# Four stages in one program: where the last rows of a stage are normalised, and how the gate and up weights are loaded

## The chip, the cores and the metric

The kernel runs on one core of a Trainium2 chip. The metric is the device time of one execution in microseconds (us). The engines are TensorE (PE; its weight loads are shown apart as PEld), VectorE (DVE), ScalarE (ACT), GpSimd (POOL) and SyncE (SP, which here only issues DMAs and counts up semaphores); each runs its own queue of instructions in order and waits for the others by semaphores.

## The reference, cut to what matters

64 sequences of 64 tokens, width 256, go through two decoder layers of three sublayers each; after every sublayer the sum with its input is layer-normalised over the 256 columns.

```python
x = _layernorm(x + _L0_attn_ref(x, Wq, Wk, Wv, Wo))           # 16 heads of 128
x = _layernorm(x + _L0_xattn_ref(x, ctx_2048, ...))           # 16 heads, context and own rows
x = _layernorm(x + _L0_ffn_ref(x, w_gate, w_up, w_down))      # silu(x @ gate) * (x @ up) @ down, hidden 1024
x = _layernorm(x + _L1_attn_ref(x, ...))                      # 4-bit weights and activations
x = _layernorm(x + _L1_xattn_ref(x, ctx_2048, ctx_2048, ...))
x = _layernorm(x + _L1_ffn_ref(x, input2, scale, scale1))     # fp8 product
```

`_layernorm` subtracts the mean and divides by the square root of the variance plus 1e-5.

## The kernel before

All 4096 rows of x lie in SBUF as 32 tiles of 128 rows (`sh.x`, 128 partitions x 32 x 256). `program` (L3449) runs four stages one after the other: `self_attention_block` (A, 2 tiles per turn, 16 turns), `cross_attention_block` (B, 1 tile per turn, 32 turns), `gated_mlp_block` (C, 4 tiles per turn, 8 turns) and `tail_block` (D, all three sublayers of the second layer, 2 tiles per turn). Each stage is a block with its own instruction queues: all engines meet at its end before the next begins. The order inside a turn is written out by hand per engine (`turn`), and two or three turns overlap; the first and last turns are unrolled, the others are a loop.

The end of a turn is the same in A, B and C. `residual` (L104) adds the last projection to `sh.x` on VectorE into a buffer `res`; `row_stats` (L113) makes `bn_stats` and `bn_aggr` of each tile on VectorE; `normalise` (L130) makes five GpSimd steps: variance plus epsilon, the power -0.5, mean times that, rows times that, rows minus the shift, written back to `sh.x`. The buffers are `sh.res` (two tiles) in A and B, and `WideRows` (four tiles, allocated inside C) in C. For the last turn all of this stands at the end of the stage.

At its start B loads a context tile and its weights, VectorE lays out rotary tables, and GpSimd counts up 50 semaphores (L1168). C issues three loads of 1 MB each (`w_gateT`, `w_upT`, `w_downT`, L1318), counts up its semaphores on SyncE (L1320), copies four tiles of x (L1432), turns them on TensorE (L1330) and takes a high and a low part; ScalarE makes the high part of each weight (`split_high`, L66), VectorE the low part (`split_low`, L73), for three whole pieces in a row. `gate_up(i, j)` multiplies hidden columns 128 j to 128 j + 127; the first two (j = 0, 1) run before the loop once both gate and up are ready, the rest once `w_down` is. The last turn of C also rounds the second layer's weights (`sh.quantised`).

D first loads tile 0 and 1 of x and `of_chunk` by DMA (L1700, L1701). TensorE multiplies the value bias by the output weights (L1749), VectorE adds the output bias (L2254), TensorE waits for `of_chunk_ready` and turns x (L1762). Each turn starts with a chain that goes from engine to engine: `lowest` and `highest` (L2269, L2263, VectorE), `find_bias`, `halve_bias`, `find_spans` (L3022 to L3038, GpSimd), `widest` (L2282), `turn_cmax` (TensorE), `find_top`, `thresholds` (L2314), `exceed` (L2329, VectorE), `weigh_steps` (L3046, GpSimd) and on to the projections. GpSimd first clears the value buffers of both attentions (L2998 to L3013).

## Time and profile before

| | us |
|---|---|
| median of 3 runs (lowest, highest) | 2766.9 (2765.09, 2777.92) |
| the profiled execution | 2765.4 |
| its span in the trace | 2763.6 |
| TensorE busy (share of the span) | 2625.6 (95%) |
| VectorE busy | 1911.1 (69%) |
| ScalarE busy | 1413.9 (51%) |
| GpSimd busy | 1183.4 (43%) |
| the 16 DMA engines, mean rate | 18 GB/s |

The profile is of one execution. Busy times are shares of the whole span, over four stages with different limits; a busy TensorE is not TensorE at its peak. PEclk is the TensorE clock that was granted, as a share of 2.4 GHz (0.50 is 1.2 GHz). Times in the timeline are counted from the start of the span; "idle before" is how long the engine had nothing to do ahead of that line, and the arrow names what released it.

### The profile page before, as it was taken

The numbers are of one execution on the slowest core, as the hardware profiler recorded it, in microseconds if no ns is written. First come the engines' busy times: TensorE is split into PE (matmuls) and PEld (weight loads), VectorE is DVE, ScalarE is ACT, GpSimd is POOL, SyncE is SP. The second block draws the span as 40 slices with busy tenths as digits, with TensorE's granted clock in tenths as the row PEclk, the third lists the DMA queues.
The fourth block names the chain that finished last, engine by engine and source line by source line (L and its number), as shares of the span: only waits on it lengthen the run. The fifth ranks groups of instructions, "written<-read, shape, count | busy, mean of one in ns | idle before, by whom it ended". The sixth has DMA issues, their size and how long they took to land. (4 is left out here: it accounts for less than half of the span.)

```text
span 2763.6 us, 66143 instructions
## 1 busy us (share of the span) xinstructions
PE 2625.6 (95%) x23860; PEld 2277.5 (82%) x23860; DVE 1911.1 (69%) x4152; ACT 1413.9 (51%) x3352; POOL 1183.4 (43%) x1559
## 2 busy tenths in 40 slices
PE   7999999997899999999999969999699999999996
PEld 7999999995798888888988858888477777777775
DVE  6655565564777777777777745444599899867775
ACT  3222222223666666666666643332466666666664
POOL 2211111113667767767677630111234444444443
PEclk9999999998999999999999989999799999999997
DMA  5000000001000000000000020000100000001100
GB/s 192 9 8 8 4 8 8 8 0 62 5 6 4 4 6 4 4 6 4 6 4 4 4 80 1 0 0 0 39 9 13 8 11 11 20 29 43 38 30 24
DMA packets 43394, 49.65 MB, mean 18 GB/s; under 512 B 3952, under 2 KB 33616, under 8 KB 43056
## 3 DMA queue, kind: packets, MB, share of 16 engines
q1 hardware_dynamic: 43312, 48.55, 5.3%
q8 instruction: 52, 0.85, 0.1%
q14 instruction: 30, 0.25, 0.0%
HBM read 35.96 MB, written 4.19 MB: 15 GB/s over the span
## 5 line engine op out<-in xcount | busy, mean ns | idle before, releaser
L588 POOL TENSOR_TENSOR a_probs<-a_probs,a_rs 128x512 f32<-128x512 f32 x64 | 70.6, 1103 | 466.4 <-DVE a_rs L444 466.4
L1174 POOL TENSOR_TENSOR b_rows<-b_rows,b_swapped 128x512 f32<-128x512 f32 x160 | 204.7, 1288 | 56.5 <-DVE b_swapped L947 56.5
L1109 ACT ACTIVATE b_probs<-bank,b_shift,b_q_scale 128x128 f32<-128x128 f32 x512 | 228.2, 461 | 0.7
L532 ACT COPY a_pT<-bank 128x512 f32<-128x512 f32 x64 | 37.5, 586 | 308.4 <-PE bank L325 308.4
L1221 POOL TENSOR_TENSOR b_probs<-b_probs,b_rs 128x512 f32<-128x512 f32 x128 | 133.2, 1041 | 137.3 <-DVE b_rs L999 134.1
L449 DVE TENSOR_TENSOR a_oT<-bank,a_oT 128x512 fp32r<-128x512 f32 x128 | 82.5, 686 | 143.6 <-ACT a_oT L537 143.6
L955 DVE TENSOR_REDUCE b_ss<-b_squares 128x4 f32<-128x512 f32 x192 | 125.2, 680 | 73.7 <-ACT b_squares L1084 73.7
L1184 POOL TENSOR_TENSOR b_rms<-b_rms,sh_minus_half 128x8 f32<-128x8 f32 (+1 forms) x128 | 170.4, 1331 | 10.6
L46 PE MATMUL bank<-a_xT,early_wq 128*128 128x256 f32 x512 | 150.2, 293 | 13.2 <-DVE early_wq L73 10.4
L46 PE MATMUL bank<-early_wo,b_oT 128*128 128x256 f32 x512 | 150.7, 294 | 1.4 <-DVE b_oT L921 1.4
L46 PE MATMUL bank<-early_wo,a_oT 128*128 128x256 f32 x512 | 145.3, 284 | 4.0 <-DVE a_oT L449 4.0
L1096 ACT COPY b_qT<-bank 128x512 f32<-128x512 f32 x128 | 75.1, 586 | 141.6 <-PE bank L796 141.6
L48 PE MATMUL bank<-early_wo,b_oT 128*128 128x256 f32 x512 | 145.7, 285 | 0.0
L48 PE MATMUL bank<-a_xT,early_wq 128*128 128x256 f32 x512 | 145.6, 284 | 0.0
L47 PE MATMUL bank<-a_xT,early_wq 128*128 128x256 f32 x512 | 145.5, 284 | 0.0
L47 PE MATMUL bank<-early_wo,b_oT 128*128 128x256 f32 x512 | 145.1, 283 | 0.0
L48 PE MATMUL bank<-early_wo,a_oT 128*128 128x256 f32 x512 | 143.4, 280 | 0.0
L47 PE MATMUL bank<-early_wo,a_oT 128*128 128x256 f32 x512 | 143.2, 280 | 0.0
L814 PE MATMUL bank<-b_kT,b_qT 128*128 128x128 f32 x1024 | 135.5, 275 | 0.0
L1391 DVE TENSOR_TENSOR c_h<-c_silu,bank 128x512 f32<-128x512 f32 x64 | 44.0, 688 | 131.4 <-PE bank L48 128.4
L840 PE MATMUL bank<-b_pT,b_v 128*128 128x256 f32 x512 | 132.7, 382 | 1.7 <-DVE b_oT L921 1.1
L1443 ACT ACTIVATE c_silu<-bank 128x512 f32<-128x512 f32 x64 | 38.3, 598 | 183.8 <-PE bank L48 182.3
(386 smaller groups left out, 9049.0 us busy)
## 6 DMA issues: line engine op xcount, KB each, us to landing
d_x_in<-sh_x SPq DMA_DIRECT2D x32, 256.0 KB, 2.4
a_xT_in<-in_xT SPq DMA_DIRECT2D x16, 256.0 KB, 2.7
sh_x<-in_x SPq DMA_DIRECT2D x1, 4096.0 KB, 18.1
b_ctx_in<-in_ctxT SPq DMA_DIRECT2D x32, 128.0 KB, 2.0
e_cT<-in_ctxT SPq DMA_DIRECT2D x32, 128.0 KB, 2.5
out<-f_res SPq DMA_DIRECT2D x16, 256.0 KB, 2.6
a_qT<-in_L_attn_Wq SPq DMA_DIRECT2D x4, 512.0 KB, 6.2
a_stage<-in_L_attn_Wo SPq DMA_DIRECT2D x1, 2048.0 KB, 13.0
```

Of the source, the lines that this page charges most:

```text
L46: pe.matmul(out, left[0], right[0], start=start, stop=False)
L47: pe.matmul(out, left[0], right[1], start=False, stop=False)
L48: return pe.matmul(out, left[1], right[0], start=False, stop=stop)
L449: dve.tensor_tensor(of_batch(1, g, b), bO[b][:, :].rearrange("p (r h q) -> p r h q", r=2, h=R), of_batch(0, g, b).bitcast(F32), ALU.subtra ...
L814: op = pe.matmul(bS[:, o:o + 128], qT[:, g, b, 2 * p:2 * p + 2, :].rearrange("p h q -> p (h q)"), kT[:, g, b].rearrange("p a k -> p (a k)" ...
L840: op = pe.matmul(bO[:, b * 256:(b + 1) * 256], v[:, b, g * HD:(g + 1) * HD], pT[:, g % 2, b].rearrange("p h q -> p (h q)"), start=True, st ...
L955: dve.tensor_reduce(ss[:, unit, :], squares[:, unit % 2, :].rearrange("p (h e) -> p h e", h=R), AX.X, ALU.add).then_inc(summed[unit], 1)
L1096: op = act.copy(qT[:, unit - Q].rearrange("p b h q -> p h b q"), src)
L1109: op = act.activation(probs[:, g % 2, keys], bS[:, keys], ACT.Exp, bias=shift[:, g % 2, a:a + 1], scale=q_scale[:, g, a // 2, a % 2:a % 2 ...
L1174: pool.tensor_tensor(rows[:, unit, :], rows[:, unit, :], swapped[:, half, :], ALU.add).then_inc(added[unit], 1)
L1184: pool.tensor_tensor(ms, ms, sh.minus_half[:, 0:n], ALU.pow).then_inc(rms_ready[step], 1)
L1221: pool.tensor_tensor(pr, pr, rs[:, g % 2, :].unsqueeze(2).to_broadcast([128, R, 128]), ALU.mult).then_inc(probs_ready[g], 1)
```

## The change

For A, B and C the last turn's statistics and normalisation are taken out of the stage. The next stage does them at its start with two new helpers, `late_stats` (VectorE) and `late_normalise` (GpSimd): two tiles in B, one in C, four in D. In B and C, VectorE and ScalarE wait for `late_step` before the second turn (in C before `turn(0, 1, ...)`); in D, SyncE waits for the fifth step (`zeroed` at 12) before it loads x of turn 1, and GpSimd does the late rows between `find_spans` and `weigh_steps` of turn 0. `WideRows` is therefore allocated outside C.

In C the gate and up weights are loaded and split in two blocks of columns: the first 256 of each (pieces 0 and 1), then the other 768 (pieces 2 and 3), then `w_down` (piece 4), which ScalarE and VectorE split behind the first SiLU and the first gating. `w_ready` counts to 2 before `gate_up(0, 0)` and to 5 before the loop.

In D TensorE turns tiles 0 and 1 straight out of `sh.x`, the value bias product follows behind it, the output bias is added behind `centre`, TensorE's waits for `out_bias`, `of_chunk` and `first_row` move behind `turn_cmax_x` of turn 0, and the clearing of the second attention's values moves into turn 1. `f_res` now uses the place of `sh.quantised.rows`.

The diff, with allocations and some context left out:

```diff
@@ -145,6 +145,32 @@
     pool.sem_inc(norm_done, 1)
+
+
+def late_stats(dve, rows, n_tiles, done):
+
+    for r in range(n_tiles):
+        dve.bn_stats(rows.stats[:, r, :], rows.res[:, r, :]).then_inc(done, 1)
+    dve.wait_ge(done, n_tiles)
+    for r in range(n_tiles):
+        dve.bn_aggr(rows.meanvar[:, r, :], rows.stats[:, r, :]).then_inc(done, 1)
+
+
+def late_normalise(pool, rows, first_tile, n_tiles, stats_done, step, before):
+
+    n = n_tiles
+    pool.wait_ge(stats_done, 2 * n)
+    pool.tensor_scalar(rows.rstd[:, 0:n], rows.meanvar[:, 0:n, 1], LN_EPS, None, ALU.add).then_inc(step, 1)
+    pool.wait_ge(step, before + 1)
+    pool.tensor_tensor(rows.rstd[:, 0:n], rows.rstd[:, 0:n], rows.minus_half[:, 0:n], ALU.pow).then_inc(step, 1)
+    pool.wait_ge(step, before + 2)
+    pool.tensor_tensor(rows.shift[:, 0:n], rows.meanvar[:, 0:n, 0], rows.rstd[:, 0:n], ALU.mult).then_inc(step, 1)
+    pool.tensor_tensor(rows.res[:, 0:n, :], rows.res[:, 0:n, :],
+                       rows.rstd[:, 0:n].unsqueeze(2).to_broadcast([128, n, D]), ALU.mult).then_inc(step, 1)
+    pool.wait_ge(step, before + 4)
+    pool.tensor_tensor(rows.x[:, first_tile:first_tile + n, :], rows.res[:, 0:n, :],
+                       rows.shift[:, 0:n].unsqueeze(2).to_broadcast([128, n, D]), ALU.subtract).then_inc(step, 1)
+    pool.wait_ge(step, before + 5)
@@ -468,7 +494,7 @@
                         residual(dve, sh, older, 2, [b[:, 0:D] for b in bY], y_ready, res_ready, norm_done)
-                    if older is not None and g == 2:
+                    if older is not None and g == 2 and before is not None:
                         row_stats(dve, sh, older, 2, res_ready, stats_ready, meanvar_ready)
@@ -586,7 +612,7 @@
                         pool.tensor_tensor(pr, pr, rs[:, g % 2, :].unsqueeze(2).to_broadcast([128, 8, S]), ALU.mult).then_inc(probs_ready, 1)
-                    if before is not None and g == 2:
+                    if before is not None and now is not None and g == 2:
                         normalise(pool, sh, before, 2, meanvar_ready, norm_step, norm_done)
...
@@ -998,8 +1025,10 @@
-            def residual(i):
-                if i is not None:
+            def add_rows(i):
+                if type(i) is int and i == sh.turns - 1:
+                    residual(dve, sh, i, 1, [bY[:, 0:D]], y_ready, res_ready, norm_done)
+                elif i is not None:
                     residual_stats(dve, sh, i, 1, [bY[:, 0:D]], y_ready, res_ready, stats_ready, meanvar_ready, norm_done)
@@ -1009,7 +1038,7 @@
                 take_v(mid, 1)
-                residual(old)
+                add_rows(old)
                 invert(mid, 1)
@@ -1037,10 +1066,15 @@
+            def split_out_weights():
+                split_low(dve, pieces[-1], len(pieces) - 1, w_high, w_ready)
+                dve.wait_ge(late_step, 5)
+
+            late_stats(dve, sh, 2, late_stats_done)
             low_ctx(0)
...
             lay_out_tables()
-            all_turns(dve, turn, lambda: split_low(dve, pieces[-1], len(pieces) - 1, w_high, w_ready))
+            all_turns(dve, turn, split_out_weights)
@@ -1160,7 +1194,11 @@
             high_x(0)
-            all_turns(act, turn, lambda: split(2))
+
+            def split_out_weights():
+                split(2)
+                act.wait_ge(late_step, 5)
+            all_turns(act, turn, split_out_weights)
@@ -1221,7 +1259,7 @@
             def layer_norm(i):
-                if i is not None:
+                if i is not None and not (type(i) is int and i == sh.turns - 1):
                     normalise(pool, sh, i, 1, meanvar_ready, norm_step, norm_done)
...
@@ -1277,9 +1321,11 @@
         wd = sb("wd", [128, 2, J, D], F32R)
-        pieces = (to_split(wg, full[0][:, :].rearrange("p (c n) -> p c n", c=C), 1)
-                  + to_split(wu, full[1][:, :].rearrange("p (c n) -> p c n", c=C), 1)
-                  + to_split(wd, full[2][:, :].rearrange("p (j n) -> p j n", j=J), 1))
+        front, rest = slice(0, F // 4), slice(F // 4, F)
+        columns = [("w_gateT", front), ("w_upT", front), ("w_gateT", rest), ("w_upT", rest), ("w_downT", slice(0, D))]
+        pieces = [(w[:, 0, :, block], w[:, 1, :, block], full[n][:, :].rearrange("p (c n) -> p c n", c=C)[:, :, block])
+                  for block in (front, rest) for n, w in enumerate((wg, wu))]
+        pieces += to_split(wd, full[2][:, :].rearrange("p (j n) -> p j n", j=J), 1)
         sh.quantised.round_in(full[0][:, :].rearrange("p (m c n) -> p m c n", m=4, c=C))
...
@@ -1304,7 +1351,7 @@
         n_turns = sh.turns // NR
-        wide = WideRows(sh, sb, NR)
+        wide = sh.wide
         block = ctx.enter_context(nc.Block())
@@ -1314,8 +1361,8 @@
         def _(sp):
-            for n, name in enumerate(("w_gateT", "w_upT", "w_downT")):
-                sp.dma_start(pieces[n][2], t[name].rearrange("(c p) n -> p c n", p=128)).then_inc(w_loaded[n], 16)
+            for n, (name, block) in enumerate(columns):
+                sp.dma_start(pieces[n][2], t[name].rearrange("(c p) n -> p c n", p=128)[:, :, block]).then_inc(w_loaded[n], 16)
             for s in looped:
@@ -1374,7 +1421,7 @@
             gate_up(0, 1)
-            pe.wait_ge(w_ready, 3)
+            pe.wait_ge(w_ready, 5)
             turns_of(pe, turn)
@@ -1415,15 +1462,17 @@
+            late_stats(dve, sh, 1, late_stats_done)
             low_x(0)
-            for n, piece in enumerate(pieces):
-                split_low(dve, piece, n, w_high, w_ready)
+            for n in range(4):
+                split_low(dve, pieces[n], n, w_high, w_ready)
             gated(0, 0)
+            split_low(dve, pieces[4], 4, w_high, w_ready)
+            dve.wait_ge(late_step, 5)
             turn(0, 1, None, True)
...
             turn(n_turns - 1, None, n_turns - 2)
-            row_stats(dve, wide, n_turns - 1, NR, res_ready, stats_ready, meanvar_ready)
@@ -1468,15 +1517,19 @@
             take_x(0)
-            for n, piece in enumerate(pieces):
+            for n in range(4):
                 act.wait_ge(w_loaded[n], 16)
-                split_high(act, piece, w_high)
+                split_high(act, pieces[n], w_high)
             gate(0, 0)
+            act.wait_ge(w_loaded[4], 16)
+            split_high(act, pieces[4], w_high)
+            act.wait_ge(late_step, 5)
             turns_of(act, turn)
...
         def _(pool):
-            with pool.Fori(0, n_turns) as i:
+            late_normalise(pool, sh, NT - 1, 1, late_stats_done, late_step, 0)
+            with pool.Fori(0, n_turns - 1) as i:
                 normalise(pool, wide, i, NR, meanvar_ready, norm_step, norm_done)
@@ -1668,7 +1721,7 @@
         f_outer = f_sb("outer", [128, 512], BF16)
-        f_res = f_sb("res", [128, 2, 2, D])
+        f_res = sh.quantised.rows[:, 0:2]
         f_stats, f_meanvar = f_sb("stats", [128, 2, 6]), f_sb("meanvar", [128, 2, 2, 2])
@@ -1703,6 +1756,8 @@
             sh.eight.load(sp, t)
+            sp.wait_ge(zeroed, 12)
+            sp.wait_ge(x_loaded, nth(0, 1, 1, 16))
             with sp.Fori(1, n_turns) as i:
@@ -1745,22 +1800,31 @@
             pe.wait_ge(w_loaded, 16 * sh.quantised.N_LOADS)
-            for c in range(C):
-                op = pe.matmul(bP[:, 0:D], v_bias[:, c:c + 1].to_broadcast([128, 128]), w[:, O, c, :], start=(c == 0), stop=(c == C - 1))
-            op.then_inc(v_bias_through, 1)
+
+            def is_first(i):
+                return i is not None and type(i.n) is int and i.n == 0
+
+            def carry_v_bias():
+                for c in range(C):
+                    op = pe.matmul(bP[:, 0:D], v_bias[:, c:c + 1].to_broadcast([128, 128]), w[:, O, c, :], start=(c == 0), stop=(c == C - 1))
+                op.then_inc(v_bias_through, 1)
...
                     return
-                pe.wait_ge(x_loaded, nth(i.n, 1, 1, 16))
+                rows = sh.x if is_first(i) else x_in
+                if not is_first(i):
+                    pe.wait_ge(x_loaded, nth(i.n, 1, 1, 16))
                 past(pe, scaled, i, -3)
...
                     for c in range(C):
-                        op = pe.transpose(bX[0][:, c * 256 + r * 128:c * 256 + (r + 1) * 128], x_in[:, r, c * 128:(c + 1) * 128], sh.ident[:, :])
+                        op = pe.transpose(bX[0][:, c * 256 + r * 128:c * 256 + (r + 1) * 128], rows[:, r, c * 128:(c + 1) * 128], sh.ident[:, :])
                 op.then_inc(qx.turned, 1)
+                if is_first(i):
+                    carry_v_bias()
@@ -1925,6 +1989,10 @@
                 turn_cmax_x(new)
+                if is_first(new):
+                    pe.wait_ge(out_bias_ready, 9)
+                    pe.wait_ge(of_chunk_ready, 1)
+                    pe.wait_ge(zeroed, 7)
                 turn_cmax_att(old)
@@ -1950,9 +2018,6 @@
             pe.wait_ge(w_ready, 4)
-            pe.wait_ge(out_bias_ready, 1)
-            pe.wait_ge(of_chunk_ready, 1)
-            pe.wait_ge(zeroed, 7)
@@ -2242,16 +2307,19 @@
             pe.wait_ge(g_w_loaded, 16 * sh.grouped.N_LOADS)
-            pe.wait_ge(zeroed, 10)
+            pe.wait_ge(zeroed, 15)
             from_first_to_second()
...
         def _(dve):
+            late_stats(dve, sh.wide, sh.wide.N, out_bias_ready)
             dve.wait_ge(w_loaded, 16 * sh.quantised.N_LOADS)
-            dve.wait_ge(v_bias_through, 1)
-            dve.tensor_tensor(out_bias[:, :], bP[:, 0:D], b_out[:, :], ALU.add).then_inc(out_bias_ready, 1)
+
+            def carry_bias():
+                dve.wait_ge(v_bias_through, 1)
+                dve.tensor_tensor(out_bias[:, :], bP[:, 0:D], b_out[:, :], ALU.add).then_inc(out_bias_ready, 1)
@@ -2424,6 +2492,8 @@
                 centre(new, qx, bX[0])
+                if new is not None and type(new.n) is int and new.n == 0:
+                    carry_bias()
                 shift(mid, 4)
@@ -3007,12 +3077,17 @@
             pool.wait_ge(zeroed, 7)
-            pool.memset(g_v[:, :, :, :, :], 0.0).then_inc(zeroed, 1)
-            pool.wait_ge(zeroed, 8)
-            for h in range(2):
-                pool.memset(g_v[h * S:(h + 1) * S, :, :, :, 2 * W + h:2 * W + h + 1], 1.0).then_inc(zeroed, 1)
             pool.wait_ge(w_loaded, 16 * sh.quantised.N_LOADS)
-            pool.wait_ge(zeroed, 10)
+
+            def is_turn(i, n):
+                return i is not None and type(i.n) is int and i.n == n
+
+            def clear_values():
+                pool.memset(g_v[:, :, :, :, :], 0.0).then_inc(zeroed, 1)
+                pool.wait_ge(zeroed, 13)
+                for h in range(2):
+                    pool.memset(g_v[h * S:(h + 1) * S, :, :, :, 2 * W + h:2 * W + h + 1], 1.0).then_inc(zeroed, 1)
+                pool.wait_ge(zeroed, 15)
@@ -3146,6 +3221,10 @@
                 find_spans(new, qx)
+                if is_turn(new, 0):
+                    late_normalise(pool, sh.wide, NT - sh.wide.N, sh.wide.N, out_bias_ready, zeroed, 7)
+                if is_turn(new, 1):
+                    clear_values()
                 weigh_steps(new, qx)
@@ -3456,6 +3535,7 @@
             sh.quantised, sh.grouped, sh.eight = QuantisedWeights(nc, late), GroupedWeights(nc, late), EightBitWeights(nc, late)
+            sh.wide = WideRows(sh, nc, late)
             for sublayer in REST:
...
                     sublayer(nc, sh)
```

## Rows read from the trace of the kernel before

**Rows 1.** Windows over the three joints: us, busy of each engine (instructions), PEclk, DMA, GB/s.

```profile
664.00:714.00 50.00, 27.57 (x118) 21.02 (x117) 26.40 (x54) 18.74 (x41) 20.51 (x22) 0.76 0.24 76
...
1635.00:1663.00 28.00, 11.97 (x47) 9.57 (x46) 12.15 (x12) 12.60 (x13) 2.16 (x5) 0.70 0.59 196
...
1934.00:1980.00 46.00, 21.61 (x164) 15.93 (x166) 17.39 (x43) 12.04 (x24) 15.11 (x28) 0.63 0.16 51
```

**Rows 2.** Timeline at joint A-B: start, us, engine, line, operation, count [idle before <-releaser].

```profile
664.42 0.42 DVE L109 TENSOR_TENSOR sh_res<-bank,sh_x 128x256 f32<-128x256 f32 x1 [0.91 <-PE bank L48]
...
668.49 1.04 POOL L144 TENSOR_TENSOR sh_x<-sh_res,sh_shift 128x512 f32<-128x512 f32 x1 [0.18 <-POOL sh_res L140]
...
670.61 0.40 ACT L1060 COPY b_x_in<-sh_x 128x256 f32<-128x256 f32 x1 [11.23 <-PEq L3455]
```

**Rows 3.** Timeline at joint B-C.

```profile
1635.47 0.42 DVE L109 TENSOR_TENSOR sh_res<-bank,sh_x 128x256 f32<-128x256 f32 x1 [4.63 <-PE bank L48]
...
1638.78 0.61 POOL L144 TENSOR_TENSOR sh_x<-sh_res,sh_shift 128x256 f32<-128x256 f32 x1 [0.18 <-POOL sh_res L140]
...
1641.43 0.39 SPq L1318 DMA_DIRECT2D c_full_g<-in_w_gateT  x1
```

**Rows 4.** Timeline at joint C-D.

```profile
1933.25 1.42 DVE L109 TENSOR_TENSOR c_res<-bank,sh_x 128x256 f32<-128x256 f32 x4 [0.75 <-PE bank L48]
...
1936.50 0.23 POOL L135 TENSOR_SCALAR c_rstd<-c_meanvar 128x4 f32<-128x4 f32 x1 [22.28 <-DVE c_meanvar L121]
...
1940.24 1.89 POOL L144 TENSOR_TENSOR sh_x<-c_res,c_shift 128x1024 f32 x1 [0.26 <-POOL c_res L140]
...
1943.19 0.60 SPq L1700 DMA_DIRECT2D d_x_in<-sh_x  x1
```

**Rows 5.** Timeline of the start of C, in order of time.

```profile
1642.99 1.04 ACT L1432 COPY c_x_in<-sh_x 128x1024 f32<-128x1024 f32 x1 [12.87 <-SPq L1320]
...
1645.92 1.49 DVE L1385 TENSOR_TENSOR c_xT<-bank,c_xT 128x512 fp32r<-128x512 f32 x2 [9.22 <-ACT c_xT L1438]
...
1646.58 1.90 ACT L66 CAST c_wg<-c_full_g 128x2048 fp32r<-128x2048 f32 x1
...
1649.08 1.90 ACT L66 CAST c_wu<-c_full_u 128x2048 fp32r<-128x2048 f32 x1 [0.61 <-DMA c_full_u<-in_w_upT]
...
1651.01 2.29 DVE L73 TENSOR_TENSOR c_wu<-c_full_u,c_wu 128x2048 fp32r<-128x2048 f32 x1 [0.21 <-ACT c_wu L66]
...
1653.36 0.79 PE L46 MATMUL bank<-c_xT,c_wg 128*128 128x512 f32 x1 [7.31 <-DVE c_wu L73]
...
1657.84 0.40 PE L46 MATMUL bank<-c_xT,c_wg 128*128 128x512 f32 x1
...
1658.10 0.69 DVE L1391 TENSOR_TENSOR c_h<-c_silu,bank 128x512 f32<-128x512 f32 x1 [1.78 <-PE bank L48]
...
1660.57 0.39 PE L46 MATMUL bank<-c_xT,c_wg 128*128 128x512 f32 x1
```

**Rows 6.** Timeline of the start of D, in order of time.

```profile
1946.46 0.11 POOL L3008 MEMSET d_first_row<- 1x32 f32 x1
...
1950.05 0.69 DVE L2269 TENSOR_REDUCE d_qx_lo<-bank 128x16 f32<-128x512 f32 x1 [4.23 <-PE bank L1762]
...
1951.52 0.22 POOL L3022 TENSOR_TENSOR d_qx_up<-d_qx_hi,d_qx_lo 128x16 f32<-128x16 f32 x1 [3.30 <-DVE d_qx_hi L2263]
...
1958.74 0.22 DVE L2314 TENSOR_TENSOR d_qx_thr<-d_qx_top_rows,qw_powers 128x56 f32<-128x56 f32 x1 [1.74 <-ACT d_qx_top_rows L2731]
```

**Rows 7.** Timeline in a turn of C: GpSimd and VectorE at once.

```profile
1703.76 1.89 POOL L144 TENSOR_TENSOR sh_x<-c_res,c_shift 128x1024 f32 x1 [0.26 <-POOL c_res L140]
...
1703.81 2.39 DVE L1395 TENSOR_TENSOR c_hT<-c_h,c_hT 128x512 fp32r<-128x512 f32 x1
```

**Rows 8.** GpSimd at the start of B: line L1168's events, and its first work.

```profile
L1168 POOLq EVENT_SEMAPHORE  x50: 17/17/17, 670.6 to 674.4; - x50
...
678.16 0.20 POOL L1182 TENSOR_SCALAR b_rms<-b_ss 128x4 f32<-128x4 f32 x1 [8.63 <-DVE b_ss L955]
```

11 lines of the change are left out of this document (9 added, 2 removed).

## The prediction

> **What bounds the kernel now.** I name the four stages A (self-attention), B (cross-attention), C (gated MLP) and D (tail). Read first the table: TensorE is busy in 95% of the span, so inside a stage almost any work of another engine is hidden. Then the windows laid over the three joints [rows 1]: there TensorE is busy in 27.57 of 50, 11.97 of 28 and 21.61 of 46 us, at a mean granted clock of 0.76, 0.70 and 0.63 of 2.4 GHz. So 63 us of idle TensorE lie around three joints, and the change touches nothing else. Then the timelines at the joints: each stage ends with the same short chain on otherwise idle engines: the last projection, the residual sum on VectorE, its row statistics, five GpSimd steps, the barrier, the first work of the next stage. The reader is to see that the next stage begins 1 to 2 us after GpSimd's last step [rows 2 to 4], and that the residual sum, the last thing that needs TensorE's product, was over 5.5 to 8.5 us before that beginning.
>
> **The joints.** The change lets each stage end with the residual sum and puts statistics and normalisation into the next one. What the end loses is the distance from the end of the last residual to the end of the last GpSimd step:
> - A-B: 664.84 to 669.53, 4.7 us; B starts 1.1 later [rows 2].
> - B-C: 1635.89 to 1639.39, 3.5 us; C starts 2.0 later [rows 3].
> - C-D: 1934.67 to 1942.13, 7.5 us; D starts 1.1 later [rows 4].
>
> I take the delay from last work to first work (1.1, 2.0, 1.1) as unchanged when VectorE instead of GpSimd is last. No row shows that case; TensorE and ScalarE are done earlier at all three, so VectorE is next late. Together 15.7 us. Bounds: nothing of it (the barrier costs what it costs whoever is last, rival 2) and 15.7.
>
> **What B takes in.** VectorE gets two statistics and two aggregates ahead of its first subtraction. Four tiles take 1.8 us at C-D, from the last residual to the first GpSimd step [rows 4]; two take about 1 us. They stand where VectorE has nothing to do until the first context tile is loaded and cast; no row shows that wait, so I bound it by 0 and 1.0 and take 0, since VectorE's first work in C also comes 4.5 us after the first load was issued [rows 3, 5]. GpSimd is tighter: it first counts up 50 semaphores, 3.8 us, and then stands free until 7.6 us after the stage's start [rows 8]. Statistics and normalisation of two tiles took 4.7 in all [rows 2], so the GpSimd part is about 3.5 and ends at about +7.4. Cost 0, at most 0.7 if it slips. The new waits of VectorE and ScalarE on `late_step` stand at the end of B's first turn, behind the split of `wo`; what is queued behind them is the second turn, and GpSimd, in program order, has then long done the late rows.
>
> **What C gains and pays.** Count from C's first DMA, 1641.43 [rows 3]. Now x is copied at +1.6, held by the counts that SyncE makes (L1320) behind three load issues; the low half of x is done at +6.0, ScalarE begins the gate weights at +5.2, and `w_up`'s low half is ready just ahead of +11.9, when the first product starts [rows 5]. Now there are five issues before the counts, two more at about 0.5 us: x is 1.0 later throughout. ScalarE starts on weights at +6.2; a quarter piece costs it 0.5 and VectorE 0.6 to 0.7 (a quarter of 1.90 and 2.29, plus start-up). Both front pieces are split at +8.3: TensorE starts 3.6 earlier. The first 24 products cover columns 0 to 255, exactly the front block, and take 7.2 us, to +15.5. By then the rest must be ready: ScalarE casts the two 3/4 pieces (1.4 each) to +10.0, does the first SiLU at +11.3, casts `w_down` (1.9) to +13.7; VectorE has the rest low at +12.1, waits for the first up product (4.7 after the start, as 1658.10 stands to 1653.36), does the gating to +13.7 and `w_down` (2.3) to +16.1. TensorE therefore waits 0.6 and goes on at +16.1 instead of +19.1 (1660.57): gain 3.0. The loads don't hold this: `w_up` landed at +7.6 [rows 5], and its second part is wanted at +8.7. Bounds: 1 to 3.6. GpSimd's late row ends by +4 and nobody wants it.
> The Trainium skill (DMA: Bandwidth & Descriptors, Bandwidth) speaks against cutting loads: batch DMAs to 1 MiB or more. By that rule the front pieces of 256 KB would land late; no row here shows a load of a column block in C, and with 8 us from issue to use I give the rule no term.
>
> **What D gains and pays.** Count from 1943.19. Now TensorE turns x only after the v bias product and the cast of `of_chunk`; VectorE's first reduction follows at +6.9, GpSimd's `find_bias` at +8.3 [rows 6]. After the change TensorE turns x straight out of `sh.x` at once; VectorE does four statistics and aggregates (1.8) and then the two reductions, to +3.3; GpSimd's memsets end at +3.4 (the 1946.46 row), those of the second half moved to turn 1. So `find_bias` runs at +3.5: gain 4.8. `of_chunk` and the v bias are wanted only behind the column maxima; `of_chunk` is cast before +6.9 (it stands ahead of the reduction at 1950.05), and the maxima themselves, on TensorE, come after `find_bias` and its three followers. Then four tiles are normalised on GpSimd: 5.6 us, 1936.50 to 1942.13 [rows 4], from +4.8 to +10.4. Behind them waits `weigh_steps`, which needs VectorE's thresholds: those come 7.2 after `find_bias` (1951.52 to 1958.74), so at +10.7, and GpSimd's work about 0.6 later. It fits with less than 1 us to spare. SyncE waits for the same rows before it loads x of turn 1, which is turned a whole turn later. The moved memsets took under 5.0 us (1946.57 to 1951.52) and now stand in the gap of turn 1 that is 7.2 in turn 0. Term 4.8, bounds 2.5 (the thresholds held up, below) and 5.
> What could eat it is seen in C: while GpSimd ran 1.89 us from 1703.76, a VectorE operation with both inputs in SBUF, begun 0.05 later, took 2.39 [rows 7]: it stood still until GpSimd was through. VectorE's thresholds are of that kind and stand 0.3 us behind the new GpSimd work; if they meet its last operation the cost is up to 1.9.
> The Trainium skill (SBUF — State Buffer, SBUF: two separate sides) calls this an exclusive lock, held for the whole instruction. The row agrees; by the rule the sum would be 21.6 where the two meet and 23.5 where they don't.
>
> **The sum.** 15.7 + 3.0 + 4.8 = 23.5 us. The profiled execution took 2765.4 (span 2763.6), the median of the three runs is 2766.9: 2741.9 against the one, 2743.4 against the other. I give 2743.
>
> **Rivals.**
> 1. The starts give nothing: the first turns of C and D are held by something that doesn't move (weights, the half clock, GpSimd behind the late rows), and only the joints count: 2766 - 15.7 = 2750. For it: three margins under 1 us. Against: each chain was followed step by step, and none of its waits is on the clock of the loads.
> 2. The change doesn't do what it says: the barriers are not led by GpSimd, and only the starts gain: 2766 - 7.8 = 2758. Against: at two joints the delay after GpSimd's last step is the same 1.1 us.
> 3. The clock pays too. TensorE's clock is granted at half (1.2 GHz) after each joint: twelve products took 4.5 us there and 2.7 at 2.4 GHz [rows 5]. At A-B the time from the last residual to B's first work shrinks from 5.8 us to 1.1 [rows 2]; if the clock stays at 2.4 GHz, each of the three starts saves up to 1.8: 2743 - 5.4 = 2738.
> 4. The port. VectorE's thresholds in D meet GpSimd's last late operation and wait for it, as in [rows 7]: 2743 + 1.9 = 2745. It decides if GpSimd is 0.3 us later than worked out.
> 5. Slower. The sparse start of D keeps the half clock. At 0.63 over 46 us [rows 1] it has it back only when dense products begin; moving work around could leave it at 1.2 GHz into the following turns. By the products above (4.5 against 2.7) each us at the half clock loses 0.4; to turn 23.5 into a loss over 0.5% (13.8) it must stay there 93 us more, three to four turns, and the time is 2780. Against: the dense part of turn 0 is the same products as before.
>
> **How the numbers follow.** Forecast 2743: 0.54. Rival 1: 0.17; rival 2: 0.06; rival 3: 0.11; rival 4: 0.09; rival 5: 0.03. The range takes in the forecast with its bounds (C down to 1, D down to 2.5, B 0.7: up to 2748), rival 3 below and rival 1 above: 2736 to 2752. A measurement of this kernel can tell about 0.5% (13.8 us) from no change, so faster means under 2753: forecast and rivals 1, 3 and 4, 0.91, less 0.01; same 0.08 (rival 2 and the edge of rival 1); slower 0.02 (rival 5 in its longer form).
>
> **What would show it.** Right: the first work of B, C and D 1.1, 2.0 and 1.1 us after a VectorE residual; the first gate product of C near +8.3 and the 25th near +16; `find_bias` of D near +3.5 and thresholds near +10.7. Wrong: a wait of TensorE on `w_down` over 1 us, a VectorE threshold over 0.22 us long, GpSimd idle nowhere between the late rows and `weigh_steps`, or stage starts still tied to GpSimd.

## The result, and the profile after

| | before | after |
|---|---|---|
| median of 6 runs each, us | 2770.2 (2765.1 to 2779.0) | 2751.1 (2746.0 to 2755.0) |
| profiled execution, its span | 2765.4, 2763.6 | 2750.9, 2749.1 |
| TensorE busy | 2625.6 (95%) | 2629.0 (96%) |
| mean granted clock | 0.972 | 0.976 |

The ratio is 0.9927, 95% interval [0.9906, 0.9949]: faster by 19 us in the medians, by 14.5 in the two profiles. The prediction summed 23.5. Two further measurements of the same two kernels gave 0.9948 [0.9928, 0.9968] and 0.9936 [0.9912, 0.9959]; the medians of the changed kernel were 2752.4 and 2751.4.

The three joints after the change, in windows laid 0.5 us or less ahead of the last residual, as in [rows 1]; columns as there:

```profile
664.58:714.58 50.00, 30.46 (x132) 23.54 (x131) 30.23 (x59) 21.41 (x50) 21.86 (x24) 0.80 0.24 77
1632.45:1660.45 28.00, 17.85 (x80) 14.45 (x79) 15.52 (x19) 14.04 (x17) 2.17 (x5) 0.82 0.61 196
1926.19:1972.19 46.00, 29.76 (x273) 23.64 (x274) 26.42 (x60) 17.98 (x35) 16.57 (x32) 0.77 0.16 52
```

TensorE is busy 2.9, 5.9 and 8.2 us longer in each, and the mean granted clock is 0.80, 0.82 and 0.77 instead of 0.76, 0.70 and 0.63.

Timeline of the changed kernel at joint A-B (start, us, engine, line, operation, count, idle before), which answers to [rows 2]:

```profile
665.00 0.42 DVE L109 TENSOR_TENSOR sh_res<-bank,sh_x 128x256 f32<-128x256 f32 x1 [0.91 <-PE bank L48]
666.36 0.35 SPq L754 DMA_DIRECT2D b_ctx_in<-in_ctxT  x1
...
666.41 0.75 DVE L153 BATCH_NORM_STATS2 sh_stats<-sh_res 128x6 f32<-128x256 f32 x2 [0.99 <-PEq L3534]
...
670.16 0.40 ACT L1101 CAST b_ctxT<-b_ctx_in 128x256 fp32r<-128x256 f32 x1 [3.37 <-DMA b_ctx_in<-in_ctxT]
...
673.00 1.04 POOL L171 TENSOR_TENSOR sh_x<-sh_res,sh_shift 128x512 f32<-128x512 f32 x1
```

The same at joint B-C, as [rows 3]:

```profile
1632.92 0.42 DVE L109 TENSOR_TENSOR sh_res<-bank,sh_x 128x256 f32<-128x256 f32 x1 [4.65 <-PE bank L48]
1635.29 0.39 SPq L1365 DMA_DIRECT2D c_full_g<-in_w_gateT  x1
1635.33 0.43 DVE L153 BATCH_NORM_STATS2 sh_stats<-sh_res 128x6 f32<-128x256 f32 x1 [1.99 <-PEq L3531]
```

The same at joint C-D and in D's turn 0, as [rows 4, 6]:

```profile
1925.43 1.42 DVE L109 TENSOR_TENSOR wide_res<-bank,sh_x 128x256 f32<-128x256 f32 x4 [0.74 <-PE bank L48]
...
1927.74 1.41 DVE L153 BATCH_NORM_STATS2 wide_stats<-wide_res 128x6 f32<-128x256 f32 x4 [0.89 <-PEq L3540]
...
1931.16 0.22 POOL L3097 TENSOR_TENSOR d_qx_up<-d_qx_hi,d_qx_lo 128x16 f32<-128x16 f32 x1
...
1936.13 1.89 POOL L171 TENSOR_TENSOR sh_x<-wide_res,wide_shift 128x1024 f32<-128x1024 f32 x1
...
1936.67 1.42 DVE L2382 TENSOR_TENSOR d_qx_thr<-d_qx_top_rows,qw_powers 128x56 f32<-128x56 f32 x1 [1.31 <-ACT d_qx_top_rows L2801]
...
1944.62 0.69 DVE L2444 TENSOR_TENSOR d_kT<-bank,d_qx_top_rows 128x512 f32<-128x512 f32 x1 [3.02 <-PE bank L1895]
```

Each stage begins 0.9, 1.95 and 0.85 us after VectorE's residual, and the late statistics are its first VectorE work. The keys (`d_kT`, L2444) end D's sparse start: behind them the dense products begin. In D `find_bias` (L3097) runs 3.47 us after the stage's first work at 1927.69. The thresholds (L2382) took 1.42 us and ended 0.07 after GpSimd's last late operation (L171).

Timeline of the start of C in the changed kernel, as [rows 5]:

```profile
1637.87 1.04 ACT L1481 COPY c_x_in<-sh_x 128x1024 f32<-128x1024 f32 x1 [10.32 <-SPq L1367]
...
1641.45 0.62 ACT L66 CAST c_wg<-c_full_g 128x512 fp32r<-128x512 f32 x1
...
1641.97 0.62 ACT L66 CAST c_wu<-c_full_u 128x512 fp32r<-128x512 f32 x1
1642.20 0.68 DVE L73 TENSOR_TENSOR c_wg<-c_full_g,c_wg 128x512 fp32r<-128x512 f32 x1
...
1642.80 0.69 DVE L73 TENSOR_TENSOR c_wu<-c_full_u,c_wu 128x512 fp32r<-128x512 f32 x1
1642.87 1.47 ACT L66 CAST c_wg<-c_full_g 128x1536 fp32r<-128x1536 f32 x1 [0.27 <-DMA c_full_g<-in_w_gateT]
...
1643.54 0.79 PE L46 MATMUL bank<-c_xT,c_wg 128*128 128x512 f32 x1 [2.60 <-DVE c_wu L73]
...
1644.37 1.76 DVE L73 TENSOR_TENSOR c_wg<-c_full_g,c_wg 128x1536 fp32r<-128x1536 f32 x1 [0.89 <-ACT c_wg L66]
...
1644.75 1.48 ACT L66 CAST c_wu<-c_full_u 128x1536 fp32r<-128x1536 f32 x1 [0.41 <-DMA c_full_u<-in_w_upT]
...
1646.26 1.76 DVE L73 TENSOR_TENSOR c_wu<-c_full_u,c_wu 128x1536 fp32r<-128x1536 f32 x1
...
1648.04 1.90 ACT L66 CAST c_wd<-c_full_d 128x2048 fp32r<-128x2048 f32 x1
...
1649.97 2.29 DVE L73 TENSOR_TENSOR c_wd<-c_full_d,c_wd 128x2048 fp32r<-128x2048 f32 x1 [0.79 <-ACT c_wd L66]
...
1652.50 0.49 PE L46 MATMUL bank<-c_xT,c_wg 128*128 128x512 f32 x1 [1.39 <-DVE c_wd L73]
```

Counted from 1635.29, the first gate product comes at +8.25 and the 25th at +17.2, after TensorE waited 1.39 us for `w_down`.

Where the 14.5 us between the two profiles are, by distances from one event to the next (both kernels have the same events): A 0.6 lost; last residual of A to last residual of B 3.1 gained; to the first gating of C's turn 1 (the 9th) 5.4; rest of C 0.1 lost; last residual of C to the first keys of D (`d_kT`) 13.0 gained; from there to the first `e_xT` of D's second half **10.6 lost**; after it 4.3 gained. The prediction has no term for the 10.6, nor for the 4.3 behind it; it has the mechanism, the half clock, as its rival 5. The window over the 10.6 in the kernel before (us, busy of PE, PEld, DVE, ACT, POOL, granted clock, DMA):

```profile
1965.43:2381.42 415.99, 401.36 (x4986) 316.76 (x4987) 372.74 (x834) 272.58 (x571) 162.40 (x345) 0.95 0.03 11
```

The same window in the changed kernel:

```profile
1944.62:2371.25 426.63, 412.94 (x4986) 329.37 (x4987) 371.70 (x834) 272.78 (x572) 164.22 (x348) 0.92 0.03 11
```

The same 4986 products; VectorE and ScalarE are busy for the same time; TensorE is busy 11.6 us longer, at a mean granted clock of 0.92 against 0.95. The experiments start from there.

### The profile page after: what moved, and what is told of

The parts are those of the page before. It is cut to its first block and busy times, and to the rows that moved or that the text cites. A ratio compares the mean times of both kernels' runs of the same rounds, so it can differ in the third digit from the quotient of the medians.

```text
span 2749.1 us, 66128 instructions
## 1 busy us (share of the span) xinstructions
PE 2629.0 (96%) x23860; PEld 2284.0 (83%) x23860; DVE 1910.4 (69%) x4154; ACT 1414.8 (51%) x3354; POOL 1184.8 (43%) x1559
## 5 line engine op out<-in xcount | busy, mean ns | idle before, releaser
L614 POOL TENSOR_TENSOR a_probs<-a_probs,a_rs 128x512 f32<-128x512 f32 x64 | 70.7, 1104 | 466.7 <-DVE a_rs L470 466.7
L558 ACT COPY a_pT<-bank 128x512 f32<-128x512 f32 x64 | 37.5, 586 | 308.9 <-PE bank L351 308.9
L1222 POOL TENSOR_TENSOR b_rms<-b_rms,sh_minus_half 128x8 f32<-128x8 f32 (+1 forms) x128 | 170.6, 1333 | 10.7
L46 PE MATMUL bank<-a_xT,early_wq 128*128 128x256 f32 x512 | 150.4, 294 | 12.9 <-DVE early_wq L73 10.2
```

What stands on the lines that cost most here:

```text
L46: pe.matmul(out, left[0], right[0], start=start, stop=False)
L1222: pool.tensor_tensor(ms, ms, sh.minus_half[:, 0:n], ALU.pow).then_inc(rms_ready[step], 1)
```

## The experiments

**The kernel before, and the changed kernel twice more.** No edit.

> The kernel before, profiled a second time, as the measure for the first run. Theory 1 (half-clock stretches of the loops fall elsewhere each time): half-clock time in D's first half differs from the 41 us of the first profile by 10 us or more, and the distance from D's first work to its turn 3 differs by 2 us or more. Theory 2 (the pattern belongs to the kernel): 41 us within 7, distance within 1 us.

> The changed kernel itself, once more, to see whether the loss behind D's start belongs to it. In the first profile the gain over the kernel before was 22.1 us at the thresholds of D's first turn, 10.8 to 12.6 us in turns 3 to 9 and 14.5 us at the end, and the rows with half the granted clock cover about 65 us of D's first half against 41 before. Theory 1 (the half-clock stretches of D's loops fall elsewhere in every execution and are no property of the edit): the stage starts repeat within 0.5 us, but the place and the sum of the half-clock stretches in D's first half differ from the first profile by 10 us or more, and the time of the profiled execution moves with them (each us at half clock costs about 0.4 us). Theory 2 (the earlier start puts the dense turns of D into a pattern that keeps the clock down): the same stretches come again within a few us and the gain falls to about 11 us by turn 3 again. Time in both: about 19 us under the kernel before.

> The changed kernel unaltered, a third time, in one call with the next three as their measure. Theory (D's first half, 416 to 428 us from the keys of turn 0 to its second half for the same work, costs 0.44 us for each us in which TensorE's clock is granted at half, and which share that is changes with small shifts of D's start): the median lies between 2749 and 2755 again; the profile's distance is either near 426.6 as in the first two profiles, or, if the stretches do fall elsewhere from one execution to the next, 3 us or more below. Its half-clock time and distance lie on the line of the nine profiles (416.0 at 43.0 us, 428.3 at 70.7) within 1.5 us either way. Rival (the distance is not the clock's): off the line by more than 3 us.

(In the expectation for the late start, further down, 416.0, 417.4 and 426.6 are meant where the text has 716.0, 717.4 and 726.6.) All profiles, in us; "half" is the part of the distance in the column before it in which the granted clock was 0.5. The three kernels with a busy start and the kernel before with one have ten more products in that distance:

| kernel | A's to B's last residual | to C's 9th gating | C's last residual to first keys | first keys to second half | half | whole span |
|---|---|---|---|---|---|---|
| before | 971.1 | 56.7 | 31.2 | 416.0 | 43.0 | 2763.6 |
| before, again | 971.1 | 56.3 | 31.2 | 417.4 | 46.0 | 2763.4 |
| columns only | 969.5 | 55.3 | 31.2 | 428.3 | 70.7 | 2770.7 |
| before, busy start | 971.0 | 56.6 | 30.8 | 423.5 | 58.0 | 2769.9 |
| after | 967.9 | 51.3 | 18.2 | 426.6 | 68.1 | 2749.1 |
| after, again | 965.8 | 53.0 | 18.9 | 426.5 | 68.1 | 2747.1 |
| after, third | 964.4 | 53.3 | 18.9 | 425.0 | 65.2 | 2750.2 |
| late rows only | 965.7 | 54.2 | 18.2 | 423.0 | 60.6 | 2747.1 |
| whole loads | 967.5 | 51.3 | 18.2 | 426.6 | 68.1 | 2745.3 |
| rows behind keys | 965.6 | 51.9 | 18.2 | 418.9 | 49.1 | 2747.0 |
| late start of D | 968.3 | 53.2 | 21.0 | 417.0 | 45.8 | 2747.2 |
| busy start | 965.5 | 52.0 | 16.9 | 422.3 | 54.6 | 2740.8 |
| late rows, busy start | 965.7 | 52.6 | 16.9 | 423.5 | 58.0 | 2746.0 |
| busy C and D | 965.3 | 54.6 | 16.9 | 421.6 | 54.6 | 2745.3 |

Theory 1 in its first form (the stretches fall anywhere in each execution) missed in these profiles, and theory 2 was met: the changed kernel showed the same 68 us at half clock twice, and 65 the third time; the kernel before 43 and 46. But two or three profiles say little of all executions. The 42 runs of the kernel before that were timed beside the later ones go from 2759.8 us at a mean granted clock of 0.975 to 2780.4 at 0.967. If the half-clock time of a run is estimated as twice the missing share of the clock times the span, that is 138 to 183 us, and the time rises by 0.44 us for each of them. So the clock does differ between executions of one kernel, by more than the 25 us between the two kernels' first profiles.

The distance follows the clock: a line through the 14 profiles is 398.4 + 0.417 times the half-clock time, and none lies more than 1.1 us off. That is the form expected for the third run.

**Only the cut of the weights.** The kernel before, with this and the pieces of `gated_mlp_block`:

```diff
-            for n, name in enumerate(("w_gateT", "w_upT", "w_downT")):
-                sp.dma_start(pieces[n][2], ...)
+            for n, (name, block) in enumerate(columns):
+                sp.dma_start(pieces[n][2], ...[:, :, block])
```

> The kernel before with only the cut of the gate and up weights: five loads, five pieces, w_down split behind the first gating; no late rows, D's start as before. Theory: C's first gate product near +8.3 and the 25th near +17.2 after C's first transfer, as in the changed kernel, and 1.9 us under the kernel before. Rival (nothing is left of it at the end of C): 0.

Measured: 2768.5 against 2766.4, ratio 1.0 [0.9985, 1.0016]. That is the time of the rival (nothing left), not the 1.9 us of the theory. C's first gate product came at +8.25 as forecast, the 25th at +17.7, and C ended 1.5 to 1.8 us nearer to B's last residual than in the two profiles of the kernel before. Then D's first half, **in which not a line differs from the kernel before**, took 428.3 us instead of 416.0 and 417.4. The window over it in this kernel, columns as above:

```profile
1961.75:2390.03 428.28, 413.47 (x4986) 326.63 (x4987) 373.25 (x834) 272.48 (x572) 162.79 (x345) 0.92 0.03 11
```

So a loss of this size does not need the new start of D; this is one profile.

**Only the late rows.** The changed kernel with the three whole loads and pieces of before.

> The change without the cut of the gate and up weights: three loads, three pieces, in the old order; the late rows of all three joints and the new start of D stay. Theory (the sum by parts, as the trace of the changed kernel measured them: joints 4.8 + 3.6 + 7.7, D's start 4.8 less 1.2 at the thresholds, context load 1.7 later, C's cut 1.9): C's first gate product stands near +11.9 after C's first transfer and the 25th near +19.1, and the whole is 1.9 us slower than the changed kernel: about 17 us under the kernel before. Rival (the cut gives nothing in the end because the clock or a later wait takes it back): same time as the changed kernel, 19 us under. Rival (the cut carries more than the trace shows): 14 us under.

Measured: 2747.4, ratio 0.9929 [0.9908, 0.995]. The first gate product stood at +11.90 as forecast; the 25th came at +20.2, not +19.1, with the clock at half until +17.9. The time is 19 us under the kernel before, the first rival's number, where the changed kernel in the same measurement was 14 under (2752.4). But its six runs reach from 2744.3 to 2756.5 and the changed kernel's 18 from 2746.0 to 2760.4: what the cut is worth, 1.2 us at C's 9th gating when done alone, is smaller than what these runs can tell. That the late rows and D's new start carry nearly all of the gain, and the cut next to nothing, is what this run and the one before it show together.

**Whole loads, cut casts.**

```diff
+            for n, name in enumerate(("w_gateT", "w_upT", "w_downT")):
+                sp.dma_start(full[n]..., t[name]...).then_inc(w_loaded[n], 16)
...
-                act.wait_ge(w_loaded[n], 16)
+                act.wait_ge(w_loaded[n % 2], 16)
```

> The changed kernel with the gate and up weights loaded whole again (three loads), while the casts and subtractions stay cut by columns in the same order. In the changed kernel and its repeat the last 3/4 of the up weights landed 9.5 us after C's first transfer, in the run with three loads at 7.6. Theory (the cut of the load into column blocks makes 2 MB land 1.9 us later, and that is why the 25th gate product came at +17.2 and not at +16.1): now no cast of a 3/4 piece waits for a load, the SiLU comes by +11.5; the front piece of the up weights must wait until +7.6, so the first gate product comes near +8.9 instead of +8.3. Rival (the queue needs 9.5 us whatever the form, because five issues and x's copy come in between): up weights at +9.4 and first gate product after +10.

Timeline of this kernel at the start of C; the first transfer is at 1631.61:

```profile
1639.23 0.62 ACT L66 CAST c_wu<-c_full_u 128x512 fp32r<-128x512 f32 x1 [1.86 <-DMA c_full_u<-in_w_upT]
...
1640.63 0.79 PE L46 MATMUL bank<-c_xT,c_wg 128*128 128x512 f32 x1 [4.39 <-DVE c_wu L73]
...
1642.61 1.28 ACT L1492 ACT_TABLE_LOAD   x1
...
1644.40 1.90 ACT L66 CAST c_wd<-c_full_d 128x2048 fp32r<-128x2048 f32 x1
...
1646.33 2.29 DVE L73 TENSOR_TENSOR c_wd<-c_full_d,c_wd 128x2048 fp32r<-128x2048 f32 x1 [0.42 <-ACT c_wd L66]
...
1648.87 0.49 PE L46 MATMUL bank<-c_xT,c_wg 128*128 128x512 f32 x1 [1.01 <-DVE c_wd L73]
```

The cast of the up weights began as they landed, at +7.6, and at 7.5 to 7.7 in all six profiles with whole loads; in the eight with cut loads the cast of their last part began at 9.5 to 10.2. Its load is also issued later there, at +1.46 instead of +0.44, behind two more; what of the 2 us is the form of the blocks and what the later issue was not separated. The first gate product came at +9.0, as forecast (+8.9). But the rest missed: SiLU began at +12.3 and not by +11.5, `w_down` was ready at +17.0 and the 25th product at +17.3, as in the changed kernel. An earlier landing of the rest buys nothing, because the front piece of the up weights then comes later: ScalarE's casts (1.47 each), its table load (1.28), SiLU, the cast of `w_down` (1.90) and VectorE's part (2.29) follow each other in either form.

**The late rows of D behind the keys.**

```diff
-                if is_turn(new, 0):
-                    late_normalise(pool, sh.wide, ...)
                 weigh_steps(new, qx)
...
                 spread_k(new)
+                if is_turn(new, 0):
+                    late_normalise(pool, sh.wide, ...)
```

> The changed kernel with D's late rows on GpSimd moved from before the weighing of the thresholds to behind the spreading of the keys of turn 0; SyncE loads x of turn 1 ahead of its wait for them. Theory (the port: VectorE's thresholds took 1.42 us instead of 0.22 because GpSimd's last late operation was running): thresholds take 0.22 again and the first keys come 1.2 us earlier against D's first work, at +15.7 instead of +16.9. Rival (the thresholds are long for another reason): still 1.4 us. The late rows then run beside VectorE's maxima of turn 0 and 1; if these wait for them it shows as single VectorE operations longer by up to 1.9 us.

Timeline of this kernel from D's first work on:

```profile
1925.95 0.60 SPq L1753 DMA_DIRECT2D d_x_in<-sh_x  x1
...
1936.20 0.22 DVE L2384 TENSOR_TENSOR d_qx_thr<-d_qx_top_rows,qw_powers 128x56 f32<-128x56 f32 x1 [1.31 <-ACT d_qx_top_rows L2803]
...
1942.89 0.69 DVE L2446 TENSOR_TENSOR d_kT<-bank,d_qx_top_rows 128x512 f32<-128x512 f32 x1 [3.02 <-PE bank L1897]
...
1949.18 1.89 POOL L171 TENSOR_TENSOR sh_x<-wide_res,wide_shift 128x1024 f32<-128x1024 f32 x1
1949.40 1.28 DVE L2453 TENSOR_REDUCE d_mx<-bank 128x8 f32<-128x512 f32 x2
```

Thresholds took 0.22 us, as forecast. The keys came at +16.94, not +15.7: the thresholds started at +10.25 instead of +8.98. TensorE's clock was at half from 1930.57 to 1933.99 here, while it turned what they wait for, and at full until 1937.62 in the first profile of the changed kernel. So the wait of the thresholds for GpSimd was removed, and what that is worth at full clock wasn't seen. VectorE's maxima (L2453), two in 1.28 us beside GpSimd's last late operation, did not wait for it; they read a bank of TensorE's results, not SBUF alone as the thresholds do.

**A later start of D.**

```diff
+                if is_first(i):
+                    pe.wait_ge(zeroed, 7)
                 for r in range(2):
```

> The changed kernel in which TensorE turns the first rows of D only when GpSimd has cleared its buffers (7 steps, +3.4): all of D's turn 0 is 3.2 us later, nothing else changes. Theory (what D's first half costs hangs on where its turns fall against the half-clock stretches, and not on the edit): the distance from the keys of turn 0 to the start of D's second half, 726.6 us in both profiles of the changed kernel and 716.0 and 717.4 in those of the kernel before, changes by 3 us or more to either side, with no relation to the 3.2. Rival (the distance belongs to the new start of D): 726.6 within 1 us, and the whole ends 3.2 us later.

Measured: `find_bias` at +6.20 and the first keys at +19.7, 2.8 us later than in the changed kernel. The distance to the second half fell from 426.6 to 417.0, and the whole took 2749.0. Turn 0's keys to turn 1's keys show it in small. The window in the changed kernel:

```profile
1944.62:1972.31 27.69, 23.12 (x224) 18.15 (x224) 16.50 (x33) 16.16 (x31) 5.77 (x12) 0.75 0.03 11
```

The same window in this kernel:

```profile
1949.01:1973.12 24.11, 19.21 (x224) 14.88 (x224) 16.51 (x33) 15.85 (x31) 5.78 (x12) 0.90 0.04 13
```

The same 224 products and the same 33 VectorE operations; 27.69 us at a mean clock of 0.75, 24.11 at 0.90. What came 2.8 us later at D's start was regained by turn 1, and 6 us more after it. The rival, 426.6 and 3.2 us on the whole, is not borne out, in one profile and one run. The same holds against the prediction: over half of what D's earlier start had gained was given up here, and the end did not move. No run takes D's new start alone away, so its worth in the final time is not shown.

**TensorE kept busy at D's start.**

```diff
+            def keep_busy(n):
+                for _ in range(n):
+                    pe.matmul(bO[:, 0:D], v_bias..., w[:, O, 0, :], start=True, stop=True)
```

> The changed kernel with 31 products whose result nobody reads, put into TensorE's idle times in D's turn 0 and at the beginning of turn 1 (6 behind the v bias, 3 behind the maxima, 12 ahead of the key projection, 10 ahead of the first transposed probabilities). Theory (the sparse start is what brings the half-clock stretches of D's first 60 us, 34 to 44 us in the profiles so far): half-clock time there falls under 20 us, the keys of turn 2 stand 3 us or more nearer to D's first work, and the whole is 3 to 6 us faster than the changed kernel, near 2746. Rival (the clock does not follow this, and the added products only stand in the way): same half-clock time, whole 1 to 4 us slower.

The window from C's last residual to D's first keys in this kernel:

```profile
1923.81:1940.74 16.93, 14.69 (x94) 12.18 (x95) 9.57 (x27) 1.82 (x4) 10.78 (x20) 1.00 0.41 123
```

The same window in the changed kernel:

```profile
1926.44:1944.62 18.18, 6.76 (x52) 5.61 (x53) 9.67 (x27) 1.82 (x4) 10.80 (x20) 0.81 0.36 115
```

The clock is 1.00 instead of 0.81, and the distance 16.93 instead of 18.18, although the thresholds waited for the port (1.32 us). No half clock was granted between 1646 and 1960; of the 60 us behind D's first work 6.8 were at half clock, against 27.3 to 37.5 in the three profiles of the changed kernel. The keys of turn 2 came 68.4 us after D's first work instead of 72.1 to 74.8. But they came at 68.2 with the late start and at 67.7 with the rows behind the keys, where nothing was filled: a near turn 2 alone does not prove the filling. The whole: 2746.3 (2740.7 to 2755.0), ratio 0.9913 [0.9883, 0.9943].

**Both, and the same with C's start filled.** The second adds twelve small products behind C's first turned x.

> The change without the cut of the gate and up weights, with the 31 unread products in TensorE's idle times of D's start. It takes both single steps that came out at or below the changed kernel (2747.4 and 2746.3). Theory (clock theory; the cut of the weights is worth 0 to 2 us, far below what the clock's stretches move): within 2 us of busy_start's 2746, and D's start at the full granted clock. Rival (the cut costs time somewhere the profiles don't show, 5 us by the medians 2752.4 and 2747.4): 2741 or less. Rival (the cut is worth its 1.9 us and nothing is hidden by the clock): 2748.

> The changed kernel with the 31 unread products at D's start and 12 more at C's start, small ones (128 columns) between the turned x and the first gate product. Theory (TensorE's granted clock stays down because TensorE is nearly idle at C's start): the half-clock stretch there, 10 to 17 us in the profiles so far, shrinks by 3 us or more and C's second gating comes 1 to 4 us earlier against the last residual of B; whole 1 to 3 us below busy_start. Rival (small sparse products don't raise the granted clock, and the stretch is set by the idle time of the joint): same stretch, whole within 1 us of busy_start.

2746.3, ratio 0.9917 [0.9895, 0.9939], and 2747.6, ratio 0.9918 [0.9895, 0.994]. The first lies on busy_start's time: the rival that lets the cut cost 5 us (2741) is not borne out, and a cut worth 1.9 (2748) is within what six runs leave open. In the second the stretch at C's start was 6.8 us instead of 10.2, or of 13.7 in busy_start, but another of 6.8 came at 1648.36, when the dense products began, and the 9th gating was 1.3 to 3.3 us later than in the three profiles of the changed kernel. The first gate product came at +8.70 instead of +8.25, behind the added ones. The next 23 then ran faster, and the 25th waited all the longer for `w_down`, as this row of busy_both shows:

```profile
1648.99 0.79 PE L46 MATMUL bank<-c_xT,c_wg 128*128 128x512 f32 x1 [3.25 <-DVE c_wd L73]
```

It came at +17.7, as in the kernels with nothing filled in C. So C's start hangs on the casts of the weights there, and a better clock has nothing to shorten: the theory was right in its first half, wrong in what it brings, and the whole was not below busy_start.

The 17 runs of the three kernels with a busy start average 2746.5 us, the 18 of the changed kernel 2751.7: 5 us, and the best version found. They were timed in different measurements; the ratios, each against the kernel before beside it, say the same (0.9913, 0.9917 and 0.9918 against 0.9927, 0.9948 and 0.9936). In the profiles the 5 us are C's last residual to D's first keys, 16.9 against 18.2 to 18.9, and the distance behind it, 422.5 against 426.0 on average.

**The kernel before with a busy start.**

> The kernel before with the same 31 unread products in D's turn 0 and turn 1, without any part of the change. Theory (what busy_start gained is the clock's and has nothing to do with the late rows): D's first stretch at half clock, 30.7 us in both profiles of the kernel before, is cut to under 20 us, the keys of turn 2 come 2 to 5 us earlier against C's last residual, and the whole is 2 to 6 us under the kernel before, 2761 to 2765. Rival (the gain hangs on the shorter idle joint that the late rows leave; with 13 us of idle TensorE before D's first turned x nothing keeps the clock up): stretch still about 30 us, whole 0 to 3 us slower.

2770.5 against 2767.1, ratio 1.0009 [0.9991, 1.0026]. The stretch at half clock was 17.1 us instead of 30.7, as the theory wanted, but the first keys came only 0.4 us earlier against C's last residual, those of turn 2 came 1.9 and 3.6 us later than in the two profiles of the kernel before instead of 2 to 5 earlier, and the whole gained nothing: the rival is right about the time and wrong about the stretch. Filling brought 5 us behind the short joint and nothing behind the long one; why it did not carry on there is open, for the distance that follows (423.5) lies inside the 416.0 to 428.3 that the same code of D took unfilled.

## Why the prediction was right, and where it was wrong

**The joints: right.** From last residual to the next stage's first work it was 6.19, 5.96 and 8.94 us, and is 1.38, 2.37 and 1.25 (within 0.03) in all profiles with late rows: 4.8, 3.6 and 7.7, together 16.1 where 15.7 were summed. VectorE as the last engine leaves the delay as it was: rival 2 is out.

**What B takes in: the rows cost nothing; the rest is the load and the clock.** GpSimd's late rows ended 7.7 us after B's start and nobody waited. But the first context tile was cast 2.0 to 2.2 us after its load was issued in the four profiles without late rows, and after 1.9 to 3.8 in the ten with them; the first profile of the changed kernel is the 3.8. It gained 3.1 from A to B, the other two, with loads of 2.1, gained 5.2 and 6.6. The load is not all of it: with loads of 2.1 and 2.7 us whole_loads and the late start of D gained 3.6 and 2.8, with one of 2.9 busy_start gained 5.6. In the first two the clock was at half for 34.1 us between the two residuals, in busy_start for 20.5, and all five profiles with 20.5 lie between 965.5 and 965.8. The prediction bounded VectorE's wait for this load at its present length; what made the load late is open.

**C's start: mechanism right, size off.** The term was 3.0, from the 25th product at +16.1. It came at 17.2, 17.3 and 17.6, at most 1.9 us ahead of the kernel before, and at the 9th gating, where the clock has its part, the cut alone was worth 1.2. The step that failed is "the loads don't hold this": I took the whole load's +7.6 for the last part of a cut one. In the first profile ScalarE waited 0.27 and 0.41 us for the two large parts and was through with their casts at +10.9 instead of +10.0; from there to `w_down` every step took what was summed, so 0.9 of the slip of 1.1 was made by then. By the page DMA: Bandwidth & Descriptors of the Trainium skill (Bandwidth), whose figures are for loads issued by GpSimd, a DMA should have 1 MiB or more to reach three quarters of the peak rate. The trace agrees in direction, with 9.5 to 10.2 against 7.5 to 7.7 for the same 2 MB; it does not show that size is the cause. And it was not the front pieces of 256 KB that were late: they had landed at +2.6 to +2.7 and +3.3 to +3.9 in the eight profiles, ahead of their cast at +6.2. Yet whole loads with cut casts gave the same +17.3, so with these casts in this order the 3.0 was not to be had in either form. TensorE's wait for `w_down` was 1.4 to 2.0 us in the three profiles, over the 1 us that the prediction names as a sign of being wrong.

**D's start: the number right, partly by luck.** Summed were 4.8 us; from D's first work the keys came at 22.24 before and at 16.9 to 17.6 after, 4.6 to 5.3. Rival 4 came true in the first profile (thresholds 1.42 us long) and again in whole_loads and in the three kernels with a busy start. In the other two profiles of the changed kernel they took 0.22, but TensorE was at half clock and they started at +10.87: they were through 0.7 later than the held ones (10.87 + 0.22 against 8.98 + 1.42). My sum had them at +10.7, which was the half-clock value without saying so. In the first profile two terms that the sum lacks nearly cancelled: at full clock `find_bias` to thresholds took 5.5 us instead of 7.2, and GpSimd took back 1.2.

**The missing term.** Joints and starts together gave 21.3, 21.1 and 22.2 us in the three profiles (56.5 and 971.1 for the kernel before). The prediction ended there; of what follows it says only that "the dense part of turn 0 is the same products as before". It did name the mechanism, in rival 5: each us at half clock costs 0.4; the slope is 0.42. What was wrong is that it was made a rival that must last three turns at a stretch. Instead it is 43 to 71 us in pieces of 3.4 to 10.2 spread over D's sixteen turns, and where they fall differs from profile to profile: 416.0 to 428.3 us for the same work. What sets where they fall is not shown.

Against the mean of the two kernels before (416.7) the changed kernel lost 8.3 to 9.9 there. Is that the change's own? Four profiles with the old start of D, one of them filled, average 421.3 (416.0 to 428.3), the five with the new one unaltered 425.6 (423.0 to 426.6). That would be 4 us for the earlier start.

But what follows, D's second half, varies too, from 377.8 to 385.2 us over the 14 profiles, again with the half-clock time in it: the 4.3 us that the first pair gained there is 12.8 against 28.1 us at half clock, and the third profile of the changed kernel took 382.1, as the kernel before did. From the first keys to the end the same groups average 802.1 and 804.5, which is 2.4 apart with a spread of 13: not settled. By the medians of 18 and 48 runs, 2751.3 and 2767.4, the change brought 16 us, 5 to 6 less than the joints and starts; where the rest of that goes stays open.

**The other rivals.** Rival 1 names 2750 and is the nearest in the number, but not in the way: both starts gave what is told above, and the time went later. The forecast's own 2743 was 8 us off, and 2751 stands in the range only because the range reached up to this rival, whose mechanism did not happen: that is luck. Rival 3, that the clock pays too, is true at the joints (half-clock time between C's last residual and the first keys 28.7 and 29.1 us before, 7 to 17 after) and is in the distances already; its opposite in D's turns outweighed it.

## What to carry over

Take what one stage needs only at its end out of the chain to the next stage: at the joint it was worth the whole distance on the engines, and it was forecast within 0.5 us. Do not sum gains at the start of a long loop whose clock comes and goes: there a start 2.8 us later left the end where it was, in one run, and the first pair of profiles lost 10 us in a stretch where the same products ran at a lower clock. Before crediting an edit with it, compare the busy time of TensorE for the same number of products, and the mean granted clock of many runs.

## What the runs showed of the hardware

- TensorE's granted clock fell to half in stretches of 3.4 us and multiples of it inside D's loop, in which TensorE was busy 96 to 97% of the time, and cost 0.417 us per us. The page TensorE: Matmul & The Clock Gate of the Trainium skill (Terms) puts the penalty at the throttled time times one minus the granted share, which is half of it here; on 14 profiles it was less. TensorE's idle time in that stretch was 13.6 to 14.8 us in the ten profiles without added products, so it can have taken up 1 us or so of the difference; the rest is open.
- Where nothing is filled, the clock fell to half 1.2 to 10.8 us behind C's last residual. With unread products in the 17 us of sparse work at D's start it stayed at 2.4 GHz until 1960; behind a joint of 9 us they cut the stretch at half clock from 30.7 to 17.1 only.
- A GpSimd operation of 1.89 us held VectorE's 0.22-us thresholds until 0.07 us after its end, in five profiles (1.32 to 1.42 us instead of 0.22). The page SBUF — State Buffer of the Trainium skill (SBUF: two separate sides) calls the shared port an exclusive lock for the whole instruction, and the trace agrees. VectorE's maxima of results in a TensorE bank kept their 0.68 us each beside the same operation, in one profile.
- The context load, issued first at B's start, was used 1.9 to 3.8 us after its issue, from one execution to the next.
